# Vision tower on one core: the plain output rows of the last three images are made inside the first two experts, and the slots of the last two images are numbered after the last comparison

## The reference

```
t = layernorm(h + attention(h))                      # 8 images x 256 rows x 256 columns
probs = softmax(t @ Wr); idx = argmax(probs)         # one expert of 8 for each row
pos = running count of the rows of that expert; kept = pos < cap      # cap = 320
disp[idx*cap + pos] += t * kept                      # 320 slots for each expert
eout = relu(disp @ W1[e]) @ W2[e]                    # 256 -> 1024 -> 256
out = layernorm(t + where(kept, eout * pmax, t))
```

## Time and profile before

| what | value |
|---|---|
| median of 3 runs | 258.96 us (258.44 to 260.87) |
| the profiled execution | 258.62 us, of which the span is 256.9 us |
| PE busy | 239.4 us (93% of the span) |
| DVE, ACT, POOL busy | 183.5, 151.9, 96.1 us |
| granted TensorE clock | 0.989 of full speed over the span |

### The profile page before, as it was taken

One profiled execution on the slowest core, in us unless ns is written; L12 is line 12 of the kernel. 1 busy time (PEld: TensorE's weight loads), 2 busy tenths in 40 slices (PEclk: granted clock), 3 DMA queues, 4 the chain that ended last, 5 costly groups with the idle time before them and its releaser, 6 DMA issues.

```text
span 256.9 us, 4971 instructions
## 1 busy us (share of the span) xinstructions
PE 239.4 (93%) x1673; PEld 222.6 (87%) x1673; DVE 183.5 (71%) x549; ACT 151.9 (59%) x346; POOL 96.1 (37%) x168
## 2 busy tenths in 40 slices
PE   6899999999999999889899999999999999999950
PEld 4899898988989898656799999999999999999940
DVE  4875496787868698886456796767967779679550
ACT  4336457686867687394745567474774747746200
POOL 6000227574554654458100025034250342503762
PEclk9999999999999999999999999999999999999995
DMA  6948654173894020221899608327082370100100
GB/s 177 297 108 262 161 171 130 39 242 127 251 397 157 19 79 3 81 82 44 239 314 313 244 0 269 112 89 274 0 276 104 108 249 4 41 4 3 54 4 0
DMA packets 28378, 35.48 MB, mean 138 GB/s; under 512 B 2780, under 2 KB 25291, under 8 KB 28354
## 3 DMA queue, kind: packets, MB, share of 16 engines
q1 hardware_dynamic: 26144, 31.71, 38.6%
q0 software_dynamic: 1792, 3.47, 3.7%
q10 hardware_dynamic: 418, 0.00, 0.1%
HBM read 26.97 MB, written 9.47 MB: 142 GB/s over the span
## 4 chain that ended last, share of the span: by engine, by line
PE 74%; DVE 7%; POOL 6%; issue 5%; ACT 3%; DMA 2%; POOLq 1%; DVEq 0%; ACTq 0%
PE bank L1236 15%; PE bank L1307 14%; PE bank L1238 14%; PE bank L1237 14%; PE bank L1323 5%; PE bank L1360 4%; PE bank L1481 3%; POOL out_dram L555 2%; DMA bqc<-in_L_attn_bq_dram 2%; PE bank L1334 2%; DVE xT L916 2%; PE bank L1532 2%; ACT tokens_mem L623 1%; POOL dispatched L515 1%; POOL yrstd L579 1%
## 5 line engine op out<-in xcount | busy, mean ns | idle before, releaser
L1153 DVE SCALAR_TENSOR_TENSOR h_lo<-bank,h_hi 128x320 fp32r<-128x320 f32 x58 | 28.3, 489 | 30.6 <-ACT h_hi L800 27.8
L800 ACT ACTIVATE h_hi<-bank 128x320 fp32r<-128x320 f32 x58 | 25.2, 437 | 38.9 <-PE bank L1238 38.9
L1236 PE MATMUL bank<-einT_hi,w_hi 128*128 128x320 f32 x128 | 40.6, 317 | 1.7 <-DVE h_lo L1153 1.4
L1238 PE MATMUL bank<-einT_hi,w_lo 128*128 128x320 f32 x128 | 39.6, 310 | 0.0
L1237 PE MATMUL bank<-einT_lo,w_hi 128*128 128x320 f32 x128 | 39.6, 309 | 0.0
L928 DVE TENSOR_TENSOR w_lo<-w_raw,w_hi 128x1024 fp32r<-128x1024 f32 x32 | 38.9, 1214 | 0.0
L555 POOL DMA_INDIRECT out_dram<-tokens_mem,images x24 | 27.7, 1154 | 29.4 <-ACT tokens_mem L817 22.2
L1236 PE MATMUL bank<-h_hi,w_hi 128*128 128x320 f32 x112 | 35.5, 317 | 0.1
L1237 PE MATMUL bank<-h_lo,w_hi 128*128 128x320 f32 x112 | 34.7, 310 | 0.0
L1238 PE MATMUL bank<-h_hi,w_lo 128*128 128x320 f32 x112 | 34.6, 309 | 0.0
L726 ACT ACTIVATE w_hi<-w_raw 128x1024 fp32r<-128x1024 f32 x32 | 33.7, 1054 | 0.0
(11 more groups left out here) (228 smaller groups left out, 575.1 us busy)
## 6 DMA issues: line engine op xcount, KB each, us to landing
w_raw<-in_L_ffn_W_dram SPq DMA_DIRECT2D x16, 1024.0 KB, 7.8
images<-in_x_dram SPq DMA_DIRECT2D x7, 768.0 KB, 4.9
dispatched<-blank SPq DMA_DIRECT2D x4, 645.0 KB, 9.2
images<-dispatched SPq DMA_DIRECT2D x9, 258.0 KB, 3.3
out_dram<-lone SPq DMA_DIRECT2D x8, 256.0 KB, 3.3
images<-in_x_dram SPq DMA_DIRECT2D x2, 384.0 KB, 5.2
images<-dispatched SPq DMA_DIRECT2D x9, 64.5 KB, 3.8
out_dram<-tokens_mem,images POOLq DMA_INDIRECT x24, 3.4
```

The source lines that it names most:

```text
L800: act.activation(hidden_halves(n)[0], bank[n % 2][:, 0:CAP], ACT.Relu).then_inc(h_hi_ready, 1)
L1153: dve.scalar_tensor_tensor(lo, bank[n % 2][:, 0:CAP], 0.0, hi.bitcast(F32), ALU.max, ALU.subtract).then_inc(h_ready, 1)
L1236: pe.matmul(to, ah, bh, start=first, stop=False)
L1238: return pe.matmul(to, al, bh, start=False, stop=last)
```

## The change

It has three parts. On ACT, `norm_lone(5)` and `norm_lone(6)` move from between the rows of images 6 and 7 into blocks 2 and 6 of expert 0, and `norm_lone(7)` moves from block 1 of expert 0 to block 2 of expert 1. On SP, their three stores move behind the weight loads of expert 2. On DVE, `assign` is cut into `compare` and `number`: the slots of image 6 are numbered after the comparisons of image 7 (`mine` gets two buffers, and `count(L)` on PE waits for the picks in place of the slots), and `late_residual` makes the statistics of each half of image 7 right after its residual.

```
-                if 2 <= i < B + 1:
+                if 2 <= i < L:
                     store_lone(i - 2)
...
-            store_lone(L)
             for e in range(2, E):
                 load_first(e)
                 load_second(e)
+                if e == 2:
+                    for b in range(L - 2, B):
+                        store_lone(b)
...
-            norm_lone(L - 2)
-            norm_lone(L - 1)
             norm_rows(L)
...
-                    if e == 0 and j == 1:
+                    if e == 0 and j in (2, 6):
+                        norm_lone(L - 2 if j == 2 else L - 1)
+                    if e == 1 and j == 2:
                         norm_lone(L)
...
+            def late_residual():
+                settle()
+                dve.wait_ge(xb_ready, L + 1)
+                dve.wait_ge(t_ready, SC * (L - 1))
+                for n, (s, at) in enumerate(((1, 5), (0, 7))):
+                    dve.wait_ge(attn_done if n else late_attn_done, L + 1 if n else 1)
+                    dve.scalar_tensor_tensor(resid[:, L % 2, s, :], bank[at][:, 0:D],
+                                             rinv[:, L % 2, s:s + 1], xb[:, L % 2, s, :], ALU.mult, ALU.add
+                                             ).then_inc(resid_ready, 1)
+                    dve.wait_ge(resid_ready, SC * L + n + 1)
+                    step(dve.bn_stats(stats[:, s, :], resid[:, L % 2, s, :]))
...
             softmax_max(L)
             moments(L - 1)
-            assign(L - 1)
+            compare(L - 1)
             softmax_sum(L)
-            residual(L)
+            late_residual()
             moments(L)
             route(L)
             factor(L - 1)
-            assign(L)
+            compare(L)
+            number(L - 1)
+            number(L)
             factor(L)
...
                 if b >= 1:
                     pe.wait_ge(tallied, b)
-                    pe.wait_ge(slot_ready, b)
+                    if b == L:
+                        pe.wait_ge(pick_ready, SC)
+                    else:
+                        pe.wait_ge(slot_ready, b)
```

More of the change, by code:

```diff
@@ L184, in vit_tower_kernel @@
         lsum = sb("lsum", [P, SC])
-        mine = sb("mine", [P, SC, E])
+        mine = sb("mine", [P, 2, SC, E])
         place = sb("place", [P, SC])
@@ L985, in residual @@
             def residual(b):
-                dve.wait_ge(late_attn_done if b == L else attn_done, 1 if b == L else b + 1)
+                dve.wait_ge(attn_done, b + 1)
                 settle()
@@ L990, in residual @@
                     dve.wait_ge(t_ready, SC * (b - 1))
-                for s, at in ((1, 5), (0, 7)) if b == L else ((0, 7), (1, 5)):
-                    if b == L and s == 0:
-                        dve.wait_ge(attn_done, b + 1)
+                for s, at in enumerate((7, 5)):
                     dve.scalar_tensor_tensor(resid[:, b % 2, s, :], bank[at][:, 0:D],
@@ L996, in residual @@
                                              ).then_inc(resid_ready, 1)
+            def late_residual():
[9 more added lines that the diff above has]
+                    step(dve.bn_stats(stats[:, s, :], resid[:, L % 2, s, :]))
             def moments(b):
-                for n, s in enumerate((1, 0) if b == L else (0, 1)):
-                    dve.wait_ge(resid_ready, SC * b + n + 1)
-                    step(dve.bn_stats(stats[:, s, :], resid[:, b % 2, s, :]))
+                if b < L:
+                    for s in range(SC):
+                        dve.wait_ge(resid_ready, SC * b + s + 1)
+                        step(dve.bn_stats(stats[:, s, :], resid[:, b % 2, s, :]))
                 if b >= 1:
@@ L1038, in factor, with compare @@
                 dve.reciprocal(trow[:, b % TR, :, D], lsum[:, :]).then_inc(factor_ready, 1)
-            def assign(b):
+            def compare(b):
                 dve.wait_ge(count_done, b + 1)
@@ L1044, in assign @@
                 count = bank[4][:, 0:SC * E].rearrange("p (s e) -> p s e", e=E)
-                step(dve.tensor_tensor(mine[:, :, :], onehot[:, b % 2], count, ALU.mult))
+                step(dve.tensor_tensor(mine[:, b % 2], onehot[:, b % 2], count, ALU.mult))
                 if b < L - 1:
@@ L1051, in assign, with number @@
                     for s in range(SC):
-                        dve.tensor_scalar(pick(b, s), slot_index, mine[:, s, 0:1], None, ALU.is_equal
+                        dve.tensor_scalar(pick(b, s), slot_index, mine[:, b % 2, s, 0:1], None, ALU.is_equal
                                           ).then_inc(pick_ready, 1)
+            def number(b):
+                if b >= L - 1:
                     step(dve.tensor_scalar(base[:, :], best[:, b % 2], -float(CAP), float(E * CAP - 1),
                                            ALU.mult, ALU.add))
-                link(dve.tensor_reduce(place[:, :], mine[:, :, :], AX_X, ALU.add))
+                link(dve.tensor_reduce(place[:, :], mine[:, b % 2], AX_X, ALU.add))
                 step(dve.tensor_scalar(over[:, :], place[:, :], float(CAP), float(NOWHERE), ALU.is_gt, ALU.mult))
@@ L1113, in _ @@
                 if i >= 1:
-                    assign(i - 1)
+                    compare(i - 1)
+                    number(i - 1)
                 softmax_sum(i)
```

## The result

| | before | changed |
|---|---|---|
| median of 4 runs | 259.91 us | 266.23 us |
| lowest to highest | 258.44 to 261.76 | 265.92 to 267.1 |
| profiled execution, its span | 258.62, 256.9 us | 265.92, 264.2 us |
| granted TensorE clock | 0.989 | 0.973 |

The ratio is 1.0245, with a 95% interval from 1.0165 to 1.0324: 6.3 us slower than these four runs of the kernel before, and 7.5 us slower than the 258.7 to 258.8 us that it took in the larger sets beside the experiments. I had forecast +1.7 us and a range up to 262.5 us. The ratios leave out executions over 1.5% above the fastest of the same kernel, which concerns three of one experiment, the lone rows alone.

What follows compares the result with a forecast made beforehand. The prediction took PE, without a gap from 133.2 us on, as the bound, so earlier waits add in full. A late store's +1.6 and +0.1 us replaced earlier gains and losses: 260.3 us profiled, 260.7 us median, range 258.4 to 262.5.

Runs made afterwards that it cites:

- the lone rows alone: The kernel before with only the change's ACT and SP parts, slots numbered where they were: 262.59 us, ratio 1.0091.
- first experiment: The changed kernel with store_lone(5) issued ahead of the weight loads of expert 2 in SP's queue: 260.26 us, ratio 1.0029.
- four buffers: The changed kernel with four buffers for `lone` instead of two, queues unchanged: 260.52 us, ratio 1.0045.
- the numbering alone: The changed kernel with ACT's and SP's parts taken back, leaving only DVE's later slot numbering and statistics in turn: 260.16 us, ratio 1.0051.

## What to carry to other kernels

Work moved off a busy engine takes its waits along: look up what frees its buffer, and where in the issuing queue that transfer now stands; behind 2 MB of weights a 256 KB store took 10.4 us. If a transfer must be late, let the wait for it stand one step further on, where the next engine has queued work: a wait to the same moment (145.0) cost PE 0.9 us in place of 3.9. And price a gap on TensorE of the length seen here, 2.8 us or more, with the clock behind it: 3 us in this kernel.

## What the runs showed of the hardware

- After 3.94 us without a product the granted clock went to 0.50 within one us of PE's new start, and came back about 7 us later. In the profiled execution with a gap of 2.76 us (the lone rows alone) it fell too. Gaps of 1.76 us and less left it at 1.00. What happens between 1.8 and 2.8 us stays open.
- An indirect DMA of POOL that begins beside a DVE operation with two SBUF inputs (1.22 us long) takes 1.58 us instead of 0.97 and lands 4.2 to 4.7 us after its start instead of 2.3 (changed kernel and first experiment against the lone rows alone, 118.63 to 120.98). Why the landing loses more than the instruction was not settled.
- W2 of expert 2 was usable 10.6 us after its issue with two stores queued right behind it (four buffers), 9.5 us after it with one store ahead and one right behind (134.61 to 144.07 in the first experiment), and 8.6 us after it with none behind (134.62 to 143.22 in the numbering alone).
